# A graph network kernel: first layer aggregates x before its matrix, and part of its sums runs inside the adjacency build

## The reference, cut to what matters

```python
for l in range(4):
    agg = jax.ops.segment_sum(x[src], dst, num_segments=n)
    h = x + agg
    h = jnp.maximum(h @ W1[l] + b1[l], 0.0)
    x = h @ W2[l] + b2[l]
```

## Time and profile before

| | us |
|---|---|
| median of 3 runs (2485.68 to 2489.79) | 2488.3 |
| the profiled execution | 2488.5 |
| its span, first to last instruction | 2486.7 |
| PE / DVE / ACT / POOL busy over the span | 1431.5 / 935.5 / 633.0 / 1366.1 |
| granted PE clock over the span | 0.756 |

### The profile page before, as it was taken

One profiled execution on the slowest core, in us unless ns is written; L12 is line 12 of the kernel. 1 busy time (PEld: TensorE's weight loads), 2 busy tenths in 40 slices (PEclk: granted clock), 3 DMA queues, 4 the chain that ended last, 5 costly groups with the idle time before them and its releaser, 6 DMA issues.

```text
span 2486.7 us, 30099 instructions
## 1 busy us (share of the span) xinstructions
PE 1431.5 (58%) x6376; PEld 930.2 (37%) x6481; DVE 935.5 (38%) x2464; ACT 633.0 (25%) x1671; POOL 1366.1 (55%) x1541
## 2 busy tenths in 40 slices
PE   4666699999988065655556165554454333343343
PEld 3333345445444053444434043433333233332333
DVE  6999622122116943223322443333333222212222
ACT  0677400000013043333333154434444000000000
POOL 1000025220211877777775677777776577777776
PEclk7888899999999587666776586667766666656556
DMA  0000001000026133333333222222222222222221
GB/s 20 0 0 0 18 14 12 6 5 1 6 49 257 37 105 102 92 105 105 106 105 96 72 78 74 71 76 76 76 75 64 65 55 55 54 54 55 55 54 46
DMA packets 120619, 148.87 MB, mean 60 GB/s; under 512 B 74779, under 2 KB 88737, under 8 KB 117362
## 3 DMA queue, kind: packets, MB, share of 16 engines
q0 software_dynamic: 40000, 81.89, 12.6%
q1 hardware_dynamic: 80562, 66.31, 8.2%
HBM read 91.39 MB, written 56.72 MB: 60 GB/s over the span
## 4 chain that ended last, share of the span: by engine, by line
POOL 45%; PE 26%; issue 17%; DVE 6%; ACT 4%; DMA 1%; POOLq 1%; SPq 0%; ACTq 0%; DVEq 0%
POOL adj L809 45%; PE acc L1053 16%; PE acc L944 4%; PE acc L1136 2%; ACT adj L1307 1%; ACT acc L1311 1%; PE acc L1200 1%; PE misc L988 1%; ACT adj L1386 1%; PE acc L1166 1%; DMA adj<-table,adj 1%; DVE feat L1605 0%; DVE adj L1936 0%; DMA table<-adj 0%; DVE adj L1971 0%
## 5 line engine op out<-in xcount | busy, mean ns | idle before, releaser
L809 POOL DMA_INDIRECT adj<-table,adj x1248 | 1235.4, 990 | 443.8 <-issue 377.9
L1200 PE MATMUL acc<-adj 128*128 x2640 | 526.8, 375 | 720.1 <-ACT adj L1386 347.5
L1200 PEld LDWEIGHTS acc<-adj 128*128 128x128 f32 x2640 | 474.9, 276 | 786.7 <-issue 786.3
L1592 DVE TENSOR_TENSOR adj<-node_iob,drel 128x384 f32<-128x384 bf16 (+1 forms) x444 | 226.3, 552 | 617.8 <-PE acc L1200 616.3
L1386 ACT ACTIVATE adj<-adj 128x128 f32<-128x128 f32 x832 | 263.1, 389 | 584.5 <-DMA adj<-table,adj 500.4
L1053 PE MATMUL acc<-adj,feat 128*128 (+2 forms) x2042 | 400.2, 353 | 6.4 <-DVEq L1641 3.3
L759 POOL TENSOR_TENSOR node_rep<-node_rep,compb 128x128 f32<-128x128 f32 x128 | 58.2, 455 | 548.0 <-DMA node_rep<-in_L_gnn_weight_dram 539.2
L1053 PEld LDWEIGHTS acc<-adj,feat 128*128 (+1 forms) x2100 | 185.6, 98 | 212.3 <-DVEq L1641 3.4
L1166 PE MATMUL acc<-adj 128*128 128x512 f32 (+1 forms) x350 | 199.1, 715 | 72.2 <-ACT adj L1401 72.2
L944 PE MATMUL acc<-feat 128*128 128x400 bf16 x625 | 142.1, 387 | 78.2 <-ACT acc L1311 68.9
L1605 DVE TENSOR_SCALAR feat<-feat 128x400 bf16<-128x400 int16 x625 | 156.9, 322 | 0.0
(11 more groups left out here) (264 smaller groups left out, 1011.4 us busy)
## 6 DMA issues: line engine op xcount, KB each, us to landing
table<-adj SPq DMA_DIRECT2D x50, 512.0 KB, 2.8
table<-adj SPq DMA_DIRECT2D x25, 1024.0 KB, 4.3
adj<-table,adj POOLq DMA_INDIRECT x1250, 2.5
table<-adj SPq DMA_DIRECT2D x25, 64.0 KB, 1.6
temp<-in_x_dram SPq DMA_DIRECT2D x6, 256.0 KB, 3.2
out_dram<-adj SPq DMA_DIRECT2D x24, 64.0 KB, 1.6
wrel<-node_rep SPq DMA_DIRECT2D x16, 64.0 KB, 3.0
adj<-in_L_gnn_W_dram SPq DMA_DIRECT2D x2, 512.0 KB, 5.2
```

Of the source, the lines that this page charges most:

```text
L809: pool.indirect_dma_start(ring[:, p_, 0:D], None, table, bass.IndirectOffsetOnAxis(ap=gidx[:, p_:p_ + 1], axis=0)).then_inc(msgs_in[u.r][c ...
L1200: last = nc.tensor.matmul(acc[:, bass.ds(blk[s], width)], hot[:, c, j, :], ring_flat[:, bass.ds(place[s], width)], start=False, stop=True, ...
L1592: return nc.vector.tensor_tensor(o, node_iob[:, :].unsqueeze(1).to_broadcast([P, n, P]), drel[:, bass.ds(s, n)].unsqueeze(2).to_broadcast( ...
```

## The change

1. The first layer sums x itself; W1 is applied to the sums after (`first_rows`, one f32 matmul of 128 x 512 per chunk). `x_columns` and `x_rows` are gone. ACT copies the sums to `hT` before `first_rows` and applies relu after it.
2. x is loaded right after `peak_set` (four DMAs) into columns of `adj` that are built late, and POOL splits it into three parts (`features_in_parts`: per chunk two casts and two subtractions), during the build.
3. Fine sums go block by block instead of in pairs: four PSUM slots of one fine block in banks 4 to 7, so banks 0 to 3 are free for the layer's `early` sums. ACT copies and zeroes 128 x 400, 196 times each.
4. DVE's operands have two buffers instead of five; an iteration is four groups (20 steps, 24 numbers to load), and there are 31 iterations.
5. From iteration 6 on, 20 iterations carry `first_sums`: behind each group of fine matmuls PE issues the three matmuls of one source block for one chunk (two blocks behind the fourth group); five iterations for each of chunks 0 to 3. DVE adds the identity for four blocks ahead of each chunk (`add_own`), and the last nine after the build.
6. After the build the first layer has only `late` left, with `turn_matrix`, `join_matrices` and `first_rows` in it.
7. The choice of the route (`peak_set`, `load_peak`, `If`) is made ahead of the build: DVE prepares two groups first, then all engines branch. POOL, too, starts x's parts there and its slices after the build; SP issues the first pair of matrices after the build.

```diff
-FG, FNB = 5, 5
-AHEAD = FG * FNB
-FSLOTS = 3
+FG, FNB, FBUF = 5, 4, 2
+FPI = FG * FNB
+AHEAD = FG * FBUF
+FSLOTS = 4
+EARLY = 4
+BPI = 5
+IPC = BLOCKS // BPI
+FIRST_AT = 6
...
+    fslots = [acc[:, (EARLY + i) * KB:(EARLY + i) * KB + FCOLS] for i in range(FSLOTS)]
...
 SP:
-            sp.wait_ge(flushed, PAIRS)
-            for c in range(CH - 1):
-                sp.dma_start(unc[:, c % 2, :, :], x[c * KB:(c + 1) * KB]...)
+                for i in range(3):
+                    sp.dma_start(xlate[:, 8 * i:8 * i + 8, :], x[8 * i * P:(8 * i + 8) * P]...).then_inc(xl_in[i], 16)
+                sp.wait_ge(xpad_set, 1)
+                sp.dma_start(xlate[0:LASTN, BLOCKS - 1, :], x[(BLOCKS - 1) * P:N]).then_inc(xl_in[3], 16)
+                sp.wait_ge(flushed, FBLOCKS)
+                matrices(0)
...
 POOL:
-            pool.wait_ge(foh_ready, FIT * FNB)
+            def features_in_parts():
+                nc.gpsimd.memset(xlate[:, BLOCKS - 1, :], 0.0).then_inc(xpad_set, 1)
+                for c in range(CH):
+                    pool.wait_ge(xl_in[c // 2], 16)
+                    nc.gpsimd.tensor_copy(p0, u).then_inc(xsplit, 1)
+                    pool.wait_ge(xsplit, 3 * c + 1)
+                    nc.gpsimd.tensor_tensor(rem, u, p0, ALU.subtract).then_inc(xsplit, 1)
+                    pool.wait_ge(xsplit, 3 * c + 2)
+                    nc.gpsimd.tensor_copy(p1, rem).then_inc(xsplit, 1)
+                    pool.wait_ge(xsplit, 3 * c + 3)
+                    nc.gpsimd.tensor_tensor(p2, rem, p1, ALU.subtract).then_inc(xparts_set, nb)
...
 PE:
+            def first_sums(c, b):
+                for s in range(PARTS3):
+                    last = nc.tensor.matmul(acc[:, c * KB:(c + 1) * KB], x3[:, s, bass.ds(b, 1), :]...,
+                                            adj[:, bass.ds(b, 1), c * KB:(c + 1) * KB]..., start=False, ...)
+            def build(m, at_, c=None):
+                (load of FPI + FNB = 24 numbers)
                 for q in range(FNB):
-                    pe.wait_ge(foh_ready, k * FNB + (q + 1))
+                    pe.wait_ge(foh_ready, m * FNB + (at_ * FNB + q + 1))
                     wait_from(pe, zeroed, turns_[q], 1)
                     for j in range(FG): (one fine matmul)
+                    if c is not None:
+                        for i in range(q, BPI if q == FNB - 1 else q + 1):
+                            if c == 0:
+                                pe.wait_ge(xparts_set, m * BPI + (i + 1))
+                            last = first_sums(c, m * BPI + i)
+            def build_and_first_sums():
+                with pe.Fori(0, FIRST_AT) as m:
+                    build(m, 0)
+                for c in range(EARLY):
+                    at_ = FIRST_AT + c * IPC
+                    pe.wait_ge(diag_set, c + 1)
+                    if c == 1:
+                        pe.wait_ge(xparts_set, BLOCKS)
+                    with pe.Fori(0, IPC - (c == EARLY - 1)) as m:
+                        build(m, at_, c)
+                build(IPC - 1, at_, EARLY - 1).then_inc(sum_ready, 1)
+                with pe.Fori(0, FIT - FIRST_AT - EARLY * IPC) as m:
+                    build(m, FIRST_AT + EARLY * IPC)
+            def first_rows(c):
+                pe.wait_ge(wmat_in, 16)
+                pe.wait_ge(hT_ready, c + 1)
+                nc.tensor.matmul(acc[:, c * KB:c * KB + chunk(c)], w1first[:, :], hT[:, c * KB:c * KB + chunk(c)], ...)
...
                     if l == 0:
-                        (x_columns, x_rows and early(0, ...) in turns)
+                        late(0, 0, 2)
+                        turn_matrix(0)
+                        late(0, 2, 4)
+                        first_rows(0)
+                        first_rows(1)
+                        join_matrices(0)
+                        first_rows(2)
+                        first_rows(3)
+                        layer_rows(0, 0)
+                        for c in range(1, 4):
+                            late(0, 4 * c, 4 * c + 4)
+                            layer_rows(0, c)
+                        late(0, 16, BLOCKS - 1)
...
 ACT, copy_out:
-                nc.scalar.activation(adj[... 2 * FB columns], fslots[r % FSLOTS], ACT.Copy)
-                nc.scalar.activation(fslots[r % FSLOTS], zerob[... 2 x FCOLS], ACT.Copy)
+                nc.scalar.activation(adj[:, :, bass.ds(i * (TURN * FB) + r * FB, FB)], fslots[r % FSLOTS]..., ACT.Copy)
+                nc.scalar.activation(fslots[r % FSLOTS], zerob[:, 0:FCOLS], ACT.Copy)
...
 DVE:
-            with dve.Fori(0, FIT) as k:
-                for q in range(FNB): (operands of a group)
+            for q in range(FBUF):
+                fine_hots(0, 0, q)
             (peak_set)
+            hold(dve, peak_set, 1)
+            peak_dve = load_peak(mybir.EngineType.DVE)
+            def build():
+                (the other groups, and ahead of iteration FIRST_AT + c * IPC:)
+                    dve.wait_ge(flushed, (c + 1) * KB // FB)
+                    add_own(4 * c, 4).then_inc(diag_set, 1)
```

More of the change, by code:

```diff
@@ L93, with last_step_of @@
 assert FULLQ == TQ - 1
+assert FIRST_AT + EARLY * IPC <= FIT and FNB <= BPI and LATE_COL + 2 * P <= NA // 2
+def last_step_of(c):
+    blocks = (c + 1) * (KB // P)
+    step = SPT * (blocks + 1) - (SPT - G)
+    return step - blocks + (c + 1) * (KB // FB)
+for c_ in range(EARLY):
+    assert last_step_of(c_) <= FPI * (FIRST_AT + IPC * c_)
 TAILN = NA - (BLOCKS - 1) * P
@@ L233, in gnn @@
         assert used[0] <= BLOCKS * NA // 2
+        late = big.rearrange("p (h w) -> p h w", h=BLOCKS)
+        xlate, xrem = (late[:, :, LATE_COL + i * D:LATE_COL + (i + 1) * D] for i in range(2))
         used[0] = 0
@@ new lines, in build @@
+                if c is not None:
+                    return last
+            def build_and_first_sums():
[11 more added lines that the diff above has]
+                    build(m, FIRST_AT + EARLY * IPC)
```

341 lines of the change are left out of this document (174 added, 167 removed).

## The result

The changed kernel takes 2472.2 us (median of 4 runs, 2469.1 to 2474.2), the kernel before 2489.0 beside it: ratio 0.9935, 95% interval 0.9921 to 0.9949. The medians lie 16.8 us apart; the interval is 13 to 20 us less. The profiled execution took 2474.2 us, its span is 2472.4.

A forecast was written before the change was run, and what follows sets the result against it. Nearly half the span is POOL's gather, only shifted; build and dense layers can move. Build ends at 354 instead of 286.45: 67.6 us lost, 82.9 gained, 15.3 net, giving 2473; 8-in-10 range 2437 to 2506.

The forecast's parts named there:

- part 1: Behind the build: the stretch to layer 0's second half falls from 129.8 us to 46.9, so 82.9 us go.
- part 2: Start of the build: branch and first load put the first fine matmul at 74.4, before 66.30, so 8.1 us lost.
- part 3: Eleven build iterations without sums: 7.9 us each, 2.0 per group instead of 1.76, because of the lost buffers.
- part 4: Twenty build iterations with sums: 8.4 us each, between 7.7 and 9.1, from PE's work, the load's gap and the sequencer's lead.
- the 5 us of the clock: Twenty iterations with sums: 5 us added for a PE clock under 1.00, moving the build's end from 327.0 to 332.
- I take 0.6: End of an iteration with sums: PE's sequencer runs 0.6 us ahead of the array, between no lead and 1.3.
- part 5: POOL's splitting beside DVE in the build: the engines hold each other up, costing 22 us, between 0 and 38.
- Rival B: POOL's splitting in the build costs DVE next to nothing: 2451 us; chance 0.25.
- Rival D: Iterations with sums: a third of the array work at half clock, 2.2 us more each, 2512 us, slower; chance 0.18.
- E: ACT's ring of four single places in the build: PE waits for ACT, 0.8 us per iteration, 2498 us; chance 0.07.
- C: Build: PE's loads are hidden behind its own queue and the loop runs at DVE's pace, 2419 us; chance 0.08.

## Why the prediction was right

The total (2473.0 against 2472.2) is closer than its parts were. Two terms of the build were off by 6 to 8 us and cancelled, and up to the first gather the trace shows a gain of 12.6 us where 15.3 were predicted; the rest of the measured 16.8 arose where nothing was changed. That the total fits so well is luck. The gain itself isn't: it rests on part 1, which the runs bear out.

- **Start of the build** (part 2): 74.4 predicted, 74.67 measured. The branch is the price: choosing the route early brought the first fine matmul 7.4 us forward.
- **Eleven iterations without sums** (part 3): 7.9 each. The changed kernel shows 7.7 to 8.6, the kernel before with two buffers 8.0 on the mean. The number is right, though it is put together otherwise than I thought: a load of 24 numbers took 1.62 us, not the 1.98 between 18 and 30, and one iteration in three starts at the lower clock (0.55 from 120.1 to 123.5, a period of 8.55 us).
- **Twenty iterations with sums** (part 4): 8.4 predicted, 8.95 measured on the mean: 179 us against 168 + 5. The first two took 10.6 and 10.5 us, together 3 more than the next two, for which the 5 us of the clock stood; the next three took 9.0 and most others 8.8. The step that failed is "I take 0.6" for the sequencer's lead. It is -0.06 in the first chunk's iterations and 0.12 behind it, because the sequencer has about 1.9 us of register operations per iteration to do between its matmuls (20 x 37 ns for the places of the fine matmuls, 20 x 56 ns for the blocks of the sums); without the second kind the lead was 1.33. That the load was 0.36 us shorter than costed paid for most of it. So a period of 8.8 is 6.65 of array work, 0.3 of waits for DVE's groups (where I had 0.1) and 1.85 of gap (where I had 2.3 - 0.6 = 1.7).
- **POOL beside DVE** (part 5): 22 predicted, 13.4 by experiment; iterations 0 to 5 took 61.7 us, not 69.4. That the two hold each other up is right and the size isn't: DVE gets six operations in beside POOL's four, 4.28 us per group instead of my 8. That DVE gets only one operation in behind each of POOL's was an estimate, and no run shows it. Both kinds of operation of a DVE group stretch (0.56 to 1.50 us, 1.25 to 2.93 for five), and the loss is unequal: a group of DVE needs 2.6 us more, four operations of POOL 0.5 more. Rival B (POOL's parts cost DVE next to nothing, 2451) falls with this.
- **End of the build**: 354 predicted, 353.9 measured. 0.3 (start) - 7.7 (POOL) + 6 (sums) + 1.3 (last five) make zero.
- **Behind the build** (part 1): 45.1 us to layer 0's second half, 47.8 measured. The 2.7 are nearly all in one row: the first 18 sums took 5.60 us, the next 18 took 3.08, at a granted clock of 0.50 (356.0 to 361.7) and 0.94 (361.7 to 364.9); in the last iterations without sums it was 0.73 on the mean (320 to 360). The 1.8 us for three `first_rows` in layer 1 were 1.9. The gain of part 1 is confirmed from the other side: 300 sums outside cost 64.9 us, inside 19.1.
- **Rival D** (the clock) is out: 1.00 from 160 to 320 us, although a gap of 1.9 us ends every iteration. PE had been busy for 29 of 40 us in the window before. **E** (ACT's ring) is out as well: ACT is busy for 28 of 40 us, its two operations at 0.493 and 0.508 us as estimated (0.51 and 0.52), and no period behind the first two is longer than 9.1. **C** (hidden loads) is out for this kernel, where the gap holds nearly the whole load; the iteration outside the loops shows how near it was, with 0.62 us of gap left.
- **Slips of working** that change little: 6.65 + 0.1 + 2.3 - 0.6 is 8.45 and not 8.4, 1 us over twenty iterations; the chances of faster add up to 0.25 + 0.08 + 0.32 = 0.65, not 0.67; POOL has 28 operations, not 25, the last four of them short.

## What to carry to other kernels

Work moved into another engine's gaps can be cheap and still leave something on the path: here 300 matmuls fell from 64.9 to 19.1 us, but every iteration then carried a register load of 1.62 us, of which 0.12 or less was covered in most of them. Count the register operations of a loop's body as well as its loads: block numbers computed from the loop's counter cost 1.1 us of the sequencer per iteration, and the one iteration that had them as constants took 7.6 us instead of 8.8. For the nineteen others that would be over 20 us, an estimate from this one period; no run tests it. Put a load where the engine waits for another anyway, in two halves if need be (11 us), and choose a route while the engines idle (7 us). A helper engine that slows down the one that bounds the stage is no free hand: POOL's splitting cost the build more (13.4 us) than the same work on the busy DVE (10.7), and both were beaten by work moved to the iterations that PE bounds.

## What the runs showed of the hardware

- A PE load of registers from SBUF took 0.59 us for 8 numbers, 0.85 for 12, 1.11 for 16, 1.62 for 24, 2.36 for 30: 0.33 for a first piece and some 0.26 for each further one, where a piece is four numbers, or a single one of those left over (30 are nine pieces). The 16 were foretold by this. Six numbers that start at a multiple of four took 0.82, as three pieces should; six that don't took 1.47, which the rule doesn't give.
- PE's matmuls followed the granted clock: a bf16 matmul of 128x512 came every 0.216 us at 1.00 (the 300 sums behind the build, 64.92 us) and every 0.43 us at 0.50 (the eight that clear the sums, 3.57 us). That is 2.4 and 1.2 columns per ns.
- PE's register operations took 37 to 84 ns each in the changed kernel. With 40 of them beside 35 matmuls the lead over the array was -0.06 to 0.12 us; with 24 it was 0.43 to 0.60; with 20, outside the loop, 1.33.
- One chip took 2746 us for the kernel that takes 2489 on others. The build isn't longer there; the gather is. Its row in the kernel with the sums behind the build, and in the changed kernel on another chip:

```profile
L834 POOL DMA_INDIRECT adj<-table,adj x1248 | 1236.3, 991 | 687.4 <-issue 374.5 <-ACT adj L1446 208.7 <-DMA table<-adj 104.2
```

```profile
L834 POOL DMA_INDIRECT adj<-table,adj x1248 | 1233.2, 988 | 443.9 <-issue 377.5 <-DMA table<-adj 64.6 <-ACT adj L1440 1.8
```

POOL issues at the same pace (991 and 988 ns) and waits 244 us longer, for buffers that ACT frees and for the table. The three other kernels on that chip show the same (687 to 704 us of waiting); what differs between the chips stays open.
